# Second cross-attention: high and low probabilities as one moving operand, and later row transfers on SyncE

## What is computed

```
# first cross-attention: 8 heads of 64, keys and values of context and latents, masked
q, k, v = heads(ln @ Wq.T), heads(concat(xn @ Wkv.T, ln @ Wlkv.T))
attn = softmax(where(mask, rmsnorm(q) * SCALE @ rmsnorm(k).T, -max))
x = x + (attn @ v) @ Wo.T + bo

# second cross-attention: 16 heads of 32, 257 keys of the context
q, k, v = heads(norm(x) @ Wq + bq), heads(ctx @ Wk + bk), heads(ctx @ Wv + bv)
weights = softmax(q @ k.T / sqrt(32))            # 32 queries x 257 keys a head
x = x + (weights @ v) @ Wo + bo
```

## Time and profile before

| | us |
|---|---|
| median of three runs | 1751.66 (1751.6 to 1756.66) |
| the profiled execution's own time | 1747.29 |
| its span | 1745.3 |

### The profile page before, as it was taken

One profiled execution on the slowest core, in us unless ns is written; L12 is line 12 of the kernel. 1 busy time (PEld: TensorE's weight loads), 2 busy tenths in 40 slices (PEclk: granted clock), 3 DMA queues, 4 the chain that ended last, 5 costly groups with the idle time before them and its releaser, 6 DMA issues. The chain is left out here.

```text
span 1745.3 us, 50134 instructions
## 1 busy us (share of the span) xinstructions
PE 1502.1 (86%) x20415; PEld 1046.4 (60%) x20415; DVE 1166.5 (67%) x2663; ACT 944.7 (54%) x2018; POOL 675.2 (39%) x824
## 2 busy tenths in 40 slices
PE   6968999999947997799999998699992699989997
PEld 3534566666535775566666666355541578778876
DVE  7858888888746887577777676377775754454441
ACT  5557888888733443355555555133334465565551
POOL 4547777777710210112221111255552333233332
PEclk9989999999979998899999999799995799999999
DMA  6121111111140000022211110300001775565512
GB/s 232 40 66 33 34 47 47 47 47 47 36 176 1 2 2 1 32 88 87 87 52 30 39 30 21 153 7 8 14 14 66 257 212 150 143 186 156 135 33 70
DMA packets 51320, 127.75 MB, mean 73 GB/s; under 512 B 8144, under 2 KB 20784, under 8 KB 51041
## 3 DMA queue, kind: packets, MB, share of 16 engines
q1 hardware_dynamic: 46066, 112.64, 19.8%
q0 software_dynamic: 5008, 11.64, 3.6%
HBM read 110.83 MB, written 15.68 MB: 72 GB/s over the span
## 5 line engine op out<-in xcount | busy, mean ns | idle before, releaser
L106 PE MATMUL e_pGU<-XT,WB 128*128 128x128 f16 x1344 | 232.2, 222 | 14.6 <-issue 9.3
L108 PE MATMUL e_pGU<-XT,WB 128*128 128x128 f16 x1344 | 232.1, 222 | 4.2 <-issue 4.2
L107 PE MATMUL e_pGU<-XT,WB 128*128 128x128 f16 x1344 | 232.1, 222 | 0.0
L2621 DVE SCALAR_TENSOR_TENSOR WB<-raw,WB 128x1024 f16<-128x1024 f32 x96 | 116.2, 1230 | 79.7 <-ACT WB L2772 79.7
L106 PEld LDWEIGHTS e_pGU<-XT,WB 128*128 128x128 f16 x1344 | 133.6, 99 | 22.0 <-issue 19.6
L108 PEld LDWEIGHTS e_pGU<-XT,WB 128*128 128x128 f16 x1344 | 133.7, 99 | 2.7 <-issue 2.7
L107 PEld LDWEIGHTS e_pGU<-XT,WB 128*128 128x128 f16 x1344 | 133.7, 99 | 1.5
L2602 POOL TENSOR_TENSOR XT<-e_mf,XT 128x256 f16<-128x256 f32 x84 | 59.0, 703 | 164.8 <-ACT XT L2786 164.7
L718 POOL TENSOR_TENSOR crn<-css,mhalf 128x8 f32<-128x8 f32 x64 | 105.8, 1654 | 5.3
L2772 ACT ACTIVATE WB<-raw 128x1024 f16<-128x1024 f32 x96 | 97.9, 1044 | 14.3 <-PE e_pY L108 13.3
L2739 DVE SCALAR_TENSOR_TENSOR e_mf<-e_pGU,e_sg 128x256 f32<-128x256 f32 x84 | 35.3, 420 | 83.9 <-ACT e_sg L2784 83.9
(11 more groups left out here) (568 smaller groups left out, 5293.2 us busy)
## 6 DMA issues: line engine op xcount, KB each, us to landing
raw<-in_WE SPq DMA_DIRECT2D x96, 512.0 KB, 4.9
raw<-in_W SPq DMA_DIRECT2D x37, 512.0 KB, 4.9
ctxin<-in_ctx SPq DMA_DIRECT2D x32, 384.0 KB, 3.3
ctxin<-in_ctxT SPq DMA_DIRECT2D x32, 384.0 KB
cv<-vlat SPq DMA_DIRECT2D x32, 96.0 KB
X<-in_x SPq DMA_DIRECT2D x8, 256.0 KB, 8.4
vlat<-vl SPq DMA_DIRECT2D x8, 256.0 KB, 2.0
dv<-vrem SPq DMA_DIRECT2D x128, 0.8 KB
```

The lines of the kernel that those rows point to most:

```text
L106: pe.matmul(out, lh, rh, start=first, stop=False, skip_group_check=shared)
L107: pe.matmul(out, lh, rl, start=False, stop=False, skip_group_check=shared)
L108: return pe.matmul(out, ll, rh, start=False, stop=last, skip_group_check=shared)
L2621: dve.scalar_tensor_tensor(WB[w][:, 1, a], ring[n][:, :], WS, WB[w][:, 0, a], ALU.mult, ALU.subtract)\
```

## The change

In `outputs` of `cross1` each value block meets the high and the low probabilities in one product where it is the high part of the values: the moving operand is `PT[:, 0:2, j, ...]`, 2 x 32 columns, and the result goes to two regions of `pO`, `pOut[:, 0]` (high) and `pOut[:, 1]` (low). The low part of the values still meets the high probabilities alone. Per row half and column block there are now 2 x 4 products instead of 3 x 4. The order is by column block, then by part. `out_sum` adds the first region and the bias, waits for its own result, and adds the second region; `d_z` is signalled by the second addition.

In `cross0` the loop over SyncE's queue issues `tail(b - 6)` behind `context(b)` instead of `tail(b - 3)`.

```diff
@@ cross0, SyncE
-            for b in range(2, B + 3):
+            for b in range(2, B + 6):
                 if b < B:
                     context(b)
-                if b - 3 >= RING:
-                    tail(b - 3)
+                if b - 6 >= RING:
+                    tail(b - 6)
@@ cross1
-        pOut = pO[:, 0, :].rearrange("p (k q) -> p k q", k=CK)
+        pOut = pO[:, 0:2, :].rearrange("p w (k q) -> p w k q", k=CK)
@@ cross1, VectorE, out_sum
-                dve.tensor_tensor(zo[:, :, :], pOut, vecs[:, VAT["bv1"]:VAT["bv1"] + CK].unsqueeze(2).broadcast_to([P, CK, S]), ALU.add)\
-                   .then_inc(sig["d_z"], 1)
+                dve.tensor_tensor(zo[:, :, :], pOut[:, 0, :, :], vecs[:, VAT["bv1"]:VAT["bv1"] + CK].unsqueeze(2).broadcast_to([P, CK, S]), ALU.add)\
+                   .then_inc(sig["d_zhalf"], 1)
+                dve.wait_ge(sig["d_zhalf"], b + 1)
+                dve.tensor_tensor(zo[:, :, :], zo[:, :, :], pOut[:, 1, :, :], ALU.add).then_inc(sig["d_z"], 1)
@@ cross1, TensorE, outputs
                 for i in range(2):
-                    for n, (a, w) in enumerate(((0, 0), (0, 1), (1, 0))):
-                        for k in range(CK):
+                    for k in range(CK):
+                        for a in range(2):
                             for j in range(BPT):
                                 h = slice((k * BPT + j) * HD1, (k * BPT + j + 1) * HD1)
-                                pe.matmul(pOut[j * HD1:(j + 1) * HD1, k, :], vb[u][:, i, a, h], PT[:, w, j, i * P + k * S:i * P + (k + 1) * S],
-                                          start=i == 0 and n == 0 and k == 0, stop=False, skip_group_check=True)
+                                pe.matmul(pOut[j * HD1:(j + 1) * HD1, 0:2 - a, k, :], vb[u][:, i, a, h],
+                                          PT[:, 0:2 - a, j, i * P + k * S:i * P + (k + 1) * S],
+                                          start=i == 0 and k == 0 and a == 0, stop=False, skip_group_check=True)
@@ the product with the last key, same function
-                        m = pe.matmul(pOut[j * HD1:(j + 1) * HD1, k, :], v3[u][:, h], PTt[:, k * S:(k + 1) * S],
+                        m = pe.matmul(pOut[j * HD1:(j + 1) * HD1, 0, k, :], v3[u][:, h], PTt[:, k * S:(k + 1) * S],
```

## The result

The changed kernel takes 1729.63 us in the median (four runs, 1728.46 to 1731.39) against 1751.63 us before: 22 us less by the medians. The comparison of runs on record gives the ratio 0.9857, 95% interval 0.984 to 0.9875. The profiled execution took 1728.52 us with a span of 1726.4. The forecast was 1725, range 1717 to 1738. One of the ten runs of experiment 7 was slow, 4498 us, and is left out.

What follows compares the result with a forecast made beforehand. TensorE's pace bounds the second cross-attention, plus waits for its own program's blocks. Products 8.0, pauses 12.2, clock 3.5, transfers 3.1, minus 0.3, make 26.5 us off the 1751.66 median: 1725, range 1717 to 1738.

Steps and rivals of the forecast that it cites:

- The pace and the dense run: Second cross-attention's outputs: 32 fewer products a batch at 7.8 ns a pair, set by issuing, save 8.0 us.
- The pauses: Second cross-attention: 256-instruction blocks executing in under 3.4 us make TensorE pause for the difference; 28.4 falls to 16.2, saving 12.2 us.
- steps 25 to 31 (94 to 82): Second cross-attention, block ends 94 to 82 instructions into scores: falling pauses of 1.9, 1.5, 1.1, 0.7 us.
- A2: Follow-up's theory for marks 94 to 34: fetch starts some 14 instructions later than forecast; 12 us of pauses, 1723 us.
- Clock: Second cross-attention: half-speed stretches begin after long pauses; fewer pauses cut their 6 us to 2.5, saving 3.5 us.
- VectorE: Second cross-attention: second addition costs nothing, 0.1 us cover left; uncovered at most 5 us; 0.3 us lost at stage's end.
- Row transfers: First cross-attention: later row transfers remove VectorE's late contexts after the first, saving 3.1 us.
- 1: Rival: pauses have another cause and stay; only 10.8 us go, 1741 us; 8%.
- 2: Rival: pairing columns saves nothing in the output burst, which stays 0.74 us; 1732 us; 10%.
- 3: Rival: VectorE becomes the pace in every second step; 5 us less gained, 1730 us; 12%.
- 4: Rival: late row transfers hold TensorE at the head of 6 quads; 1752 us up, 1760 at 10 us late; 3%.
- 5: Rival: no half-clock stretch is left and a block takes 3.2 us; 2.5 + 2.2 us more saved, 1720 us; 10%.

Runs made afterwards that it cites:

- experiment 7: Changed kernel with 96 products of 32 columns again, 450 TensorE instructions a step, both additions and later transfers kept: 1751.8 us, 0.9997 of the kernel before.
- experiment 8: Changed kernel with 40 small products ahead of the second cross-attention, all 64 products moving 64 columns: 1707.79 us, 0.9751 of the kernel before.
- experiment 2: Changed kernel with 40 small products (80 TensorE instructions) ahead of the second cross-attention's first step: 1711.63 us, 0.9766 of the kernel before.
- 3: Changed kernel with 72 small products (144 TensorE instructions) ahead of the second cross-attention's first step: 1732.47 us, 0.9797 to 0.9933 of the kernel before.
- experiment 1: The changed kernel run again, nothing altered: 1729.31 us, 0.988 of the kernel before.
- 5: Changed kernel with SyncE's row transfers as before, so the new products alone: 1726.79 us, 0.9854 of the kernel before.
- 6: Kernel before with only the row transfers three places later: 1747.45 us, 0.9976 of the kernel before.
- 11: Changed kernel with 40 small products ahead of the second cross-attention and a third VectorE pass over the sum: 1704.72 us, 0.975.
- 10: Changed kernel with 40 small products ahead of the second cross-attention and only the first of VectorE's two additions: 1705.50 us, 0.9752.

## Why the forecast was right, point by point

*The pace and the dense run.* 10.27 us were forecast for the undisturbed step and measured; 64 pairs in 0.49 us of issue were forecast as some 0.5. That issuing and not columns sets it was argued from the half-clock row; experiment 8 shows it.

*The pauses.* The mechanism is shown: moving the marks takes the pauses away without touching the work (2), moving them further brings them back (3), the old instruction count brings back the old ones (7), and each pause above 0.8 us ends 1.2 to 1.6 us after a block has landed. They stood where forecast, in odd steps, at the border of scores and keys near step 23. The largest was forecast there (2.0 us, seen 2.17); steps 25 and 29 had more, 2.28 and 2.39. The "Instruction fetch mechanics" of the Trainium skill's page "Runtime: NRT & Kernel Launch" is right on blocks of 256 instructions as far as the marks show it. That crossing one is mostly hidden holds here outside the dense run (47 packets of the queue from 730 to 1080 us, 14 waits in scores and keys), not for blocks that execute within it.

In size, 12.2 us were forecast and 8.4 saved in the changed kernel's first trace (28.4 - 20.0), but that is one execution. Experiments 1 and 5 have the same marks and 14.9 and 15.5 us of waits, and experiments 6 and 7, with the old marks, 29.5 and 29.2. The three traces with the new marks have 16.8 us in the mean, against 16.2 forecast, and the three with the old ones 29.0. So the sum came out near 12.2 in the mean, and what the steps 25 to 31 gave to it came out partly by luck. The term "steps 25 to 31 (94 to 82) 1.9, 1.5, 1.1, 0.7" has the wrong form: instead of 5.2 us in falling pauses these steps had whole ones or none, 2.28 + 1.86 + 2.39 + 2.06 = 8.6 us in the first trace, 4.3 and 4.7 us in the other two. The rule that a block's time counts from its first instruction fails when that instruction lies in the value products just ahead of the outputs. There the packet starts either ahead of those products, and nothing is lost, or only with the scores, and a whole pause follows. A later start of the fetch (A2) fits the second case alone. What decides between the two stays open; it isn't the instruction count alone, as the same kernel shows both.

*Clock.* 3.5 us forecast. What is left of the stage's excess beside the pauses of the 31 steps fell from 34.4 - 28.4 = 6.0 to 21.9 - 17.9 = 4.0 us (17.9 is 20.0 without the last scores' 2.1), so 2.0. The clock's own records have 13.7 us at 1.2 GHz in the 31 steps before and 6.8 us with the change.

*VectorE.* "The cost is nothing" was right, and so was the 0.1 us left of VectorE's own wait (0.07 in the trace of experiment 2). What the working left out is the second cover: the low probabilities end 0.3 us before the outputs that need them start. So the bound of 5 us "without that cover" was too high, and a further pass of 0.23 us cost nothing, where 2 us were expected (11). The stage's end cost 0.3 us in the first trace, as forecast, and 0.6 in that of experiment 2 (from the start of the last scores to the last sum 9.7 us before, 10.3 there).

*Row transfers.* 3.1 us forecast; 247.06 - 243.99 = 3.1 measured, and 3.3 alone (6); between single traces of the two orders it is 2.2 to 5.2. The times by themselves do not resolve it within the whole change (5 against the whole).

*The sum.* On the profiled executions 18.8 us instead of 26.5: 3.0 ahead of the stage, 20.2 in its 31 steps, minus 4.3 behind them, where the forecast had 0.3. Of those 4.3, 2.1 are the last scores' pause. On the medians it is 22.0, in the group of experiment 1 19.2. The forecast of 1725 took the sum off the median before, as the profiled execution was 4.4 us faster than it. Executions of one kernel differ by several us in stages that the change does not touch, so how near the total came (1729.6 against 1725) says less than the terms. Of the rivals, 1 is out by experiment 2, 2 by the dense run's 0.49 us, 3 by 10 and 11, 4 by 6, and 5 by the 6.8 us at half clock that stayed.

**A faster version.** The changed kernel with the 40 small products (2) beats both: 1711.63 us in its group, where the changed kernel took 1729.31 and the kernel before 1748.49.

## What to carry to other kernels

Where TensorE waits for nothing that the profile shows, count its instructions between the breaks: a fixed distance says that its program is late. The instruction queue's packets in the DMA view of narrow windows confirm it, when one lands shortly ahead of each restart. Then fewer instructions or another phase help, not faster data. A change of the instruction count moves every later break, so a gain or loss of ten microseconds can come from the count modulo 256 alone. In such a dense run at full clock a product with twice the columns can be free, as here with 64 instead of 32.

## What the runs showed of the hardware

- A block of 256 TensorE instructions that executed in about 1.2 us was followed by a pause of 1.7 to 2.5 us. Where both ends of a block lay in outputs, scores and keys and there was a pause of over 0.8 us, it took 2.9 to 3.9 us from its first instruction to the next block's.
- Such a pause ended 1.2 to 1.6 us after the 16 KB packet of the instruction queue had landed (92 pauses in nine traces); the packet itself took 0.9 to 1.5 us.
- At the same marks (94, 86, 82) the same instructions paused in some executions and not in others. The packet started with the scores in the first case, 3.0 to 3.9 us ahead of them in the second.
- Pairs of a load and a product on 128x32 tiles were issued every 7.8 ns at full clock, whether 32 or 64 columns moved, and every 10 ns at half clock when half of them moved 64. The about 25 ns that the Trainium skill's page "TensorE: Matmul & The Clock Gate" gives as the least distance (its section on the 56 ns gap) does not hold from one pair to the next on such tiles; within one of the four column groups the pairs are 4 x 7.8 = 31 ns apart, above it.
- Of the half-clock stretches within the steps of the stage none was left once the pauses were gone (granted clock 1.00 over 319 us).
